# Waits between the four indirect scatters of a batch, in an attention and mixture-of-experts kernel on one core

## The reference

```
x = x + xattn(layernorm(x), ctx, ctx)           # q, k, v, o projections with biases, softmax over 77 keys
xn = layernorm(x)
probs = softmax(xn @ router_w);  top_w, top_i = top_k(probs, 2)
out = sum over e of cw[:, e] * ((silu(xn @ gate_w[e]) * (xn @ up_w[e])) @ down_w[e])
x = x + out
```

## Time and profile before

| | |
|---|---|
| median of three runs | 1013.5 us |
| the profiled execution | 1013.09 us |
| its span, first to last instruction | 1011.3 us |
| busy in the span | PE 89%, DVE 62%, ACT 47%, POOL 29% |
| indirect scatters of rows (line 1385) | 64, 63.4 us of POOL, 990 ns each |
| granted TensorE clock, mean | 0.928 |

### The profile page before, as it was taken

The page is one execution under the profiler, slowest core; times in us unless marked ns, Lnnn a source line. Parts: engine busy times, 40 slices in busy tenths (PEclk is TensorE's granted clock), DMA queues, the critical chain, the costliest instruction groups (busy, mean ns, idle before and its releaser), DMA issues.

```text
span 1011.3 us, 32130 instructions
## 1 busy us (share of the span) xinstructions
PE 895.4 (89%) x12208; PEld 795.6 (79%) x12208; DVE 628.1 (62%) x1930; ACT 472.4 (47%) x891; POOL 290.0 (29%) x337
## 2 busy tenths in 40 slices
PE   3899888888888886199999999999999999999996
PEld 2667666666666664088999999999999999999995
DVE  7789767777777775355745644744754756644443
ACT  2677666666666674143523423532432434423221
POOL 4566733333333322502211211211212212211111
PEclk9998888888888886589999999999999999999998
DMA  4312222121211331216252522242252252222221
GB/s 144 109 42 67 61 70 65 59 59 59 59 59 59 111 120 53 93 44 179 38 151 54 152 36 54 51 137 53 33 156 53 33 156 55 33 35 36 36 32 16
DMA packets 69072, 73.57 MB, mean 73 GB/s; under 512 B 19724, under 2 KB 62810, under 8 KB 69018
## 3 DMA queue, kind: packets, MB, share of 16 engines
q1 hardware_dynamic: 44666, 32.94, 11.4%
q0 software_dynamic: 12944, 17.87, 10.2%
q10 hardware_dynamic: 11408, 22.06, 6.2%
HBM read 45.18 MB, written 26.39 MB: 71 GB/s over the span
## 4 chain that ended last, share of the span: by engine, by line
PE 50%; DMA 4%; issue 4%; DVE 3%; ACT 3%; POOL 1%; ACTq 0%; another core or an unknown queue 0%; SPq 0%; POOLq 0%; DVEq 0%
PE bank L483 11%; PE bank L485 11%; PE bank L484 11%; PE bank L681 5%; PE bank L683 5%; PE bank L682 5%; DMA raw<-expert_rows 4%; PE bank L656 1%; PE bank L544 1%; POOL expert_rows L1385 1%; DVE h_full L1252 1%; ACT h_hi L830 1%; ACT g_act L828 1%; DVE e_lo L1117 1%; ACT pt_hi L758 1%
## 5 line engine op out<-in xcount | busy, mean ns | idle before, releaser
L483 PE MATMUL bank<-xg,e_hi 128*128 128x128 f16 x2176 | 373.3, 220 | 0.7 <-DVE xg L1229 0.6
L484 PE MATMUL bank<-xg,e_hi 128*128 128x128 f16 x2176 | 373.3, 220 | 0.0
L485 PE MATMUL bank<-xg,e_lo 128*128 128x128 f16 x2176 | 373.3, 220 | 0.0
L1416 POOL DMA_INDIRECT out<-y_sb,tok_row x68 | 113.4, 1668 | 466.6 <-DVE y_sb L1247 443.1
L483 PEld LDWEIGHTS bank<-xg,e_hi 128*128 128x128 f16 x2176 | 213.5, 98 | 2.0 <-issue 0.8
L484 PEld LDWEIGHTS bank<-xg,e_hi 128*128 128x128 f16 x2176 | 213.5, 98 | 0.7
L485 PEld LDWEIGHTS bank<-xg,e_lo 128*128 128x128 f16 x2176 | 213.5, 98 | 0.0
L828 ACT ACTIVATE g_act<-bank 128x512 f32<-128x512 f32 x136 | 81.3, 598 | 249.3 <-PE bank L485 233.9
L1252 DVE SCALAR_TENSOR_TENSOR h_full<-bank,g_act 128x512 f32<-128x512 f32 x136 | 94.0, 691 | 128.7 <-ACT g_act L828 121.0
L681 PE MATMUL bank<-e_hi,h_hi 128*128 128x256 f16 x544 | 148.4, 273 | 4.1 <-DVE h_lo L1258 4.1
L683 PE MATMUL bank<-e_hi,h_lo 128*128 128x256 f16 x544 | 148.3, 273 | 0.0
(11 more groups left out here) (175 smaller groups left out, 1850.6 us busy)
## 6 DMA issues: line engine op xcount, KB each, us to landing
raw<-expert_rows SPq DMA_DIRECT2D x68, 132.5 KB, 2.5
e_stage<-in_gate_w ACTq DMA_DIRECT2D x7, 1024.0 KB
e_stage<-in_up_w ACTq DMA_DIRECT2D x7, 1024.0 KB
e_stage<-in_down_w ACTq DMA_DIRECT2D x7, 1024.0 KB
expert_rows<-pads SPq DMA_DIRECT2D x8, 530.0 KB
xin<-in_x SPq DMA_DIRECT2D x16, 256.0 KB, 2.8
xres<-in_x SPq DMA_DIRECT2D x16, 256.0 KB
out<-x SPq DMA_DIRECT2D x16, 256.0 KB
```

Of the source, the lines that this page charges most:

```text
L483: pe.matmul(dst, a_hi(c), b_hi(c), start=c == 0, stop=False)
L484: pe.matmul(dst, a_hi(c), b_lo(c), start=False, stop=False)
L485: mm = pe.matmul(dst, a_lo(c), b_hi(c), start=False, stop=ends and c == chunks - 1)
L1416: pool.indirect_dma_start(out, bass.IndirectOffsetOnAxis(tok_row[:], 0), y_sb[:], None, compute_op=ALU.add).then_inc(added, 16)
```

## The change

The second, third and fourth scatter of a batch wait until the one ahead of them has landed: the semaphore `scattered` must stand at 64 times the batch plus 16, 32 or 48. This is so only in rounds that have a batch n, so for batches 0 to 10 (rounds 5 to 15). Batches 11 to 15 are scattered as before.

```
-            def scatter(r, par):
+            def scatter(r, par, n):
...
                 for t in range(NT):
                     for k in range(2):
+                        if n and t + k:
+                            pool.wait_ge(scattered, r.value(SCATTER, 16 * (2 * t + k)))
+                            apart(pool, passed)
                         pool.indirect_dma_start(rows_dram, bass.IndirectOffsetOnAxis(slot_u[:, par, t, k:k + 1], 0),
                                                 rows[:, par, t, :], None).then_inc(scattered, 16)
...
-                    scatter(z, z.plus % 2)
+                    scatter(z, z.plus % 2, n)
```

## The result

| | before | after |
|---|---|---|
| median | 1013.8 us (1013.02 to 1018.3, 4 runs) | 977.53 us (976.2 to 979.12, 4 runs) |
| span of the profiled execution | 1011.3 us | 974.4 us |
| mean granted TensorE clock | 0.928 | 0.958 |

The ratio is 0.9635, with a 95% interval of 0.9617 to 0.9652: 36 us less, where 11 were forecast, and outside the range given (987 to 1020). The first transposes of the experts' stage are let go at 393.72 us instead of 429.72, so all of the gain is in the first stage, as expected.

What follows compares the result with a forecast made beforehand. First stage bound by a PE, ACT and DVE chain that stalls once a scatter round; 2.5 us gained less 1.2 of holds, 1.3 over nine rounds, less 1 for rounds 5 and 6: -10.7, so 1002.5 us, range 987 to 1020.

Steps and rivals of the forecast that it cites:

- The stall: Units 5 and 6 of each scatter round: back-to-back scatters hold PE's results from other engines, costing 2.24 to 2.9 us.
- Spacing and cover: POOL: scatters 3.4 us apart add 6.3 us a batch (4.6 to 7.6), covered by k_parts' 8.78 us idle time.
- k_parts has no idle time left: Sign on POOL that the forecast is wrong; it expected k_parts' idle time to fall from 8.8 to 1 to 3 us.
- Rounds 5 and 6: Cover missing there: k_parts and SP's spread come late, PE waits 2.8 us; both rounds lose 0 to 3, taken as 1.
- The holds of lone scatters: Each spaced scatter still holds PE's results at most 0.6 us; 2.4 us a round at most, half taken: 1.2 us.
- The granted clock I leave out: PE's clock in scatter rounds: 0.85 without the stall, 0.86 with it, so ending the stall does not bring it back.
- The whole stall goes, and the clock stays up: Rival, chance 0.14: lone holds meet no awaited result; 2.9 us in each of 10 rounds, less 1, giving 985 us.
- the first rival: Chance 0.20: units 5 and 6 stall from router's and slots' work or the first scatter alone, not closeness; 1014.5 us.

Runs made afterwards that it cites:

- e4_late: The kernel before, its burst of four scatters kept but started later, after unit 6's transposes; 1013.83 us, ratio 0.999.
- e3_pairs: The changed kernel with the wait for a landing left only ahead of the third scatter, so two back-to-back pairs; 981.41 us, ratio 0.9675.
- e5_paced: The changed kernel with the second to fourth scatter each waiting for the next unit's transposes instead of a landing; 971.56 us, ratio 0.9578.
- e1_fill: The kernel before with 28 unread matmuls put into unit 6 where PE stood still, scatters still back to back; 1006.26 us, ratio 0.9921.
- e1b_fill: The changed kernel with 28 unread matmuls behind unit 6's first scores; 999.95 us, ratio 0.9846.
- e9_lull: The changed kernel with three dummy ACT activations ahead of unit 5's pt_hi, which PE waits for, scatters still apart; 1017.0 us, ratio 1.0009.

## Why the prediction was wrong

The direction and the place were right, and so was the reading that scatters close together make the stall. The size was a third, because the clock was left out. Step by step:

*The stall (2.24 to 2.9 us a round; 2.24 and 0.73 make 2.97).* Right. The idle time of PE fell by 2.3 us a round, the stretch from unit 5's transposes to unit 6's by 2.96 us, pt_hi's remote waits are gone, and e4_late and e3_pairs show that they belong to scatters close together. That the trace's semaphore records have PE's posts 2.5 to 4.9 us late beside a burst (round 10) and at most 0.7 us beside scatters 2.2 us or more apart fits the reading of the earlier trace rows. What of a burst holds them is not shown by any run: e5_paced shows that nobody has to wait for the landing; close issue and overlapping transfers stay unseparated.

*Spacing and cover.* Scatters 3.3 us apart as said, the first 4.8, and 7.4 us more for POOL's batch (11.3 instead of 3.9 us from first to fourth start), the upper end of what was given. With rounds 4.5 us shorter k_parts has no idle time left, which I had named as a sign of failure; e5_paced shows that it cost nothing.

*Rounds 5 and 6.* The sum was right (0.2 us lost, 1 forecast), the parts were not: SP began to spread at 121.53, near the 120.4 worked out, but PE waited first and longest for the residual rows (5.98 us), which stand behind k_parts on POOL, and 1.18 us for k_diag. I had followed only one of the two things that POOL makes late. That it came out near is luck: round 5 gained 5 us at once, its stall and its clock, and hid the loss of round 6.

*The holds of lone scatters (1.2 us a round).* Oversized. A lone scatter does hold results, but for 0.7 us at most and mostly ones that nobody waits for. Of the ten short waits of pt_hi four lie in rounds 7 to 15 and end 1.3 us after a scatter's start, as read from the earlier trace rows; they are 0.3 to 0.4 us long, where 1.2 us in every round were taken off. Hardly any of the 1.2 us shows in PE's idle time. In nine rounds that is some 10 us of the miss.

*"The granted clock I leave out: it was 0.85 in round 4 without the stall and 0.86 with it".* This is the step that failed, and the other 20 us (9 x 2.2). I took round 4 for a round without a stall. It was one without the burst; the earlier trace rows showed its own wait of 0.73 us, and its DVE is busy 19.36 us of 22.20 beside the splitting on POOL. It could not even be counted on to have a slow clock. The same instructions with the same wait ran at full clock in other executions; from 80 to 87 us in the kernel before, and in e5_paced, which does nothing else up to there:

```profile
80.00:87.00 7.00, 7.00 (x59) 5.35 (x60) 6.90 (x27) 3.18 (x7) 5.03 (x6) 0.51 0.00 0
```

```profile
80.01 0.29 PE L483 MATMUL bank<-k_diag,q_hi 128*128 128x308 f16 x1 [0.72 <-DVE probs L994]
80.00:87.00 7.00, 5.85 (x82) 4.51 (x82) 6.86 (x28) 3.95 (x9) 5.94 (x6) 1.00 0.01 2
```

PE gets through 82 matmuls in these 7 us instead of 59, and round 5 starts 1.5 us sooner. So a wait of 0.7 us may bring the half clock or not, and which of the two is not explained by any run; the stall of 3.1 us brought it in every round. One 0.85 from round 4 says nothing of a round with the stall gone. The trace before had no such round, but the half-clock stretch right behind each stall was there to be priced: 6.8 us at 0.50 once a round. At full clock its work would be done in less time; the busy time says 2.2 us less. e1_fill, e1b_fill and e9_lull show it from three sides.

*The rivals.* "The whole stall goes, and the clock stays up" is what happened; it had 0.14, and even its 985 us counted the stall alone (29 us) and gave the clock's return no price. With 4.5 us x 9 = 40, less 1 it would have been near 974. The sentence of the Trainium skill (SBUF — State Buffer, Who interferes with whom) that PE and ACT never wait on anyone I had weighed with the first rival. What followed from it here, that the stall is not the scatters' doing, is measured to be wrong: PE's results reach the others late beside a burst, wherever the burst stands (e4_late), and PE and ACT wait for it. The sentence is about ports, and no run shows whether ports have anything to do with this.

## What to carry to other kernels

A wait of TensorE that returns in every round can cost the half clock behind it besides its own length: in unit 5 it did so in every round at 1.35 us and more, elsewhere waits of 0.7 to 1.8 us did it in some places and executions and not in others. Look in the profile for the stretches of half clock, and price a wait in front of one at both. A stretch that has another wait in it is no control for the clock. Spread indirect DMAs over the work that runs beside them, a unit apart and paced by that work, and put what POOL has to do anyway into the gaps, not behind them.

## What the runs showed of the hardware that I had not expected

- One microsecond of ScalarE ahead of a result that TensorE waits for made a round 3.0 us longer on average, 2.2 of them more busy time of TensorE; three made it 4.5 us longer. The further microseconds cost little: 23.6 us a round with two, 24.0 with three, 23.9 with the burst.
- The same wait of 0.7 us, in the same instructions, stood ahead of 6.8 us of half clock in one execution and of full clock in another.
- 28 matmuls without a use made the kernel 8 us faster (e1_fill), by keeping the clock at 1.00 across a stall.
- A memset of 2.17 us on GpSimd held a VectorE step of 0.158 us up to 2.58 us; a spacer of this kind can take back all that spacing brings.
